# Experts: the late four gated tiles leave in one accumulating store of 1 MB, ahead of GpSimd's norms of the late rows

## The reference, cut to what matters

```
x = x + tanh(g_xattn) * attention(layernorm(x), ctx, ...)      # 4 heads, 64 context rows a batch
x = x + tanh(g_ffn)   * experts(layernorm(x), ...)

experts(x):  grouped  = x.reshape(b, s // 32, 32, d)           # groups of 32 tokens
             logits   = grouped @ Wc + bc + tie                # 128 experts (32 x 4)
             perm     = (logits == max over the 32 tokens)     # each expert takes one token of each group
             permuted = perm^T @ grouped                       # gather
             inner    = relu(permuted @ W1 + b1)               # 512 -> 32 for each expert
             result   = inner @ W2 + b2                        # 32 -> 512
             out      = perm @ result                          # scatter to the tokens
```

## Time and profile before

| | us |
|---|---|
| median of 3 runs | 1733.97 |
| lowest and highest of them | 1730.71, 1737.69 |
| the profiled execution | 1737.52 |
| its span in the trace | 1735.6 |
| PE busy in the span | 1605.5 |
| POOL busy in the span | 861.4 |
| granted TensorE clock, mean | 0.987 |

### The profile page before, as it was taken

One profiled execution on the slowest core, in us unless ns is written; L12 is line 12 of the kernel. 1 busy time (PEld: TensorE's weight loads), 2 busy tenths in 40 slices (PEclk: granted clock), 3 DMA queues, 4 the chain that ended last, 5 costly groups with the idle time before them and its releaser, 6 DMA issues.

```text
span 1735.6 us, 51613 instructions
## 1 busy us (share of the span) xinstructions
PE 1605.5 (93%) x22424; PEld 1126.5 (65%) x22424; DVE 1298.3 (75%) x1893; ACT 739.4 (43%) x966; POOL 861.4 (50%) x1020
## 2 busy tenths in 40 slices
PE   8899999999999999999888998999998889898994
PEld 4677777777777777777676554666555566555662
DVE  5777777777777777777748776778777777776766
ACT  3632323233323333332234555555555455555552
POOL 3468777877787788778641233122233122233122
PEclk9999999999999999999999999999999999999998
DMA  7634545545454455545565888778888787887875
GB/s 290 176 101 151 178 141 174 165 150 164 162 187 138 164 164 163 154 158 170 164 217 174 217 218 223 213 221 202 231 222 220 211 223 191 202 229 210 225 183 153
DMA packets 180593, 325.31 MB, mean 187 GB/s; under 512 B 23056, under 2 KB 33168, under 8 KB 178960
## 3 DMA queue, kind: packets, MB, share of 16 engines
q1 hardware_dynamic: 135104, 239.15, 42.9%
q0 software_dynamic: 17616, 32.52, 11.8%
q10 hardware_dynamic: 27648, 50.34, 8.8%
HBM read 243.23 MB, written 78.71 MB: 185 GB/s over the span
## 4 chain that ended last, share of the span: by engine, by line
PE 61%; DVE 14%; DMA 12%; issue 6%; ACT 3%; POOL 2%; SPq 1%; ACTq 0%; POOLq 0%; DVEq 0%
PE ps L1493 11%; PE ps L951 11%; PE ps L998 10%; PE ps L1463 7%; PE ps L1011 5%; DMA xin<-out 5%; PE ps L1517 3%; PE ps L966 3%; PE ps L1532 3%; DMA out<-xin 3%; PE ps L1024 3%; DMA sel<-lg_scratch 2%; DVE mx L730 2%; DVE res L1405 2%; PE ps L985 2%
## 5 line engine op out<-in xcount | busy, mean ns | idle before, releaser
L184 POOL TENSOR_SCALAR xin<-xin,r_all,nb_all 128x512 f32<-128x512 f32 x128 | 113.7, 891 | 507.3 <-DMA xin<-out 379.5
L1389 DVE STREAM_TRANSPOSE res<-res 128x2048 f32<-128x2048 f32 x128 | 292.0, 2295 | 0.1
L1341 ACT ACTIVATE gat<-ps 128x1536 f32<-128x1536 f32 (+1 forms) x128 | 170.7, 1345 | 204.8 <-PE ps L1463 204.8
L951 PE MATMUL ps<-xTh,qh 128*128 128x512 f32 x512 | 210.3, 411 | 5.6 <-DVE qs L747 2.0
L951 PE MATMUL ps<-xTh,ql 128*128 128x512 f32 x512 | 201.1, 393 | 0.0
L951 PE MATMUL ps<-xTl,qh 128*128 128x512 f32 x512 | 200.5, 392 | 0.0
L1405 DVE COPY res<-ps 128x1024 f32<-128x1024 f32 x128 | 156.7, 1224 | 58.1 <-PE ps L1517 58.0
L1463 PE MATMUL ps<-sel,xin 32*128 32x128 f32 x4096 | 153.7, 285 | 36.6 <-ACT sel L215 10.3
L1312 POOL DMA_DIRECT2D out<-xin x120 | 119.9, 1124 | 97.3 <-DVE xin L1228 85.6
L552 POOL TENSOR_TENSOR xTl<-xT,xTh 128x512 fp32r<-128x512 f32 x128 | 160.5, 1283 | 12.0 <-ACT xTh L616 12.0
L1351 ACT ACTIVATE res<-ps 128x1024 f32<-128x1024 f32 x128 | 131.1, 1025 | 78.4 <-PE ps L1517 78.4
(11 more groups left out here) (169 smaller groups left out, 3288.5 us busy)
## 6 DMA issues: line engine op xcount, KB each, us to landing
gat<-in_W ACTq DMA_DIRECT2D x192, 256.0 KB, 5.6
xT<-in_xT SPq DMA_DIRECT2D x32, 1024.0 KB, 6.1
xin<-in_x SPq DMA_DIRECT2D x64, 512.0 KB, 3.8
out<-xin SPq DMA_DIRECT2D x64, 512.0 KB, 4.0
xin<-out SPq DMA_DIRECT2D x128, 256.0 KB, 4.2
xin<-in_W SPq DMA_DIRECT2D x128, 256.0 KB, 4.0
out<-xin POOLq DMA_DIRECT2D x120, 256.0 KB, 7.3
xT<-in_W SPq DMA_DIRECT2D x68, 256.0 KB, 4.5
```

The lines of the kernel that those rows point to most:

```text
L184: e.tensor_scalar(self.xn[:, t, :], self.xn[:, t, :], self.r[:, i, t:t + 1], self.nb[:, i, t:t + 1], ALU.mult, ALU.add).then_inc(self.m_xn ...
L951: last = e.matmul(ps[:, 2 + n % 2, :], a[:, c, n * DH:(n + 1) * DH], b[:, c, :], start=(k == 0), stop=(k == len(parts) - 1))
L1341: e.activation(o, v, ACT.Copy).then_inc(m_gaA.sem, 1)
L1389: e.transpose(v, v).then_inc(m_tr.sem, 1)
```

## The change

The four separate stores of the late tiles become one of 1 MB with a mark of its own, `d_yn` (`b_yn`). It waits for all four gated tiles, stands behind the wait for the W2 quarter as before, and goes out ahead of the four norms of the late rows. SP's quarters of the middle eighth of W1, and the last load of the late half, wait for that one mark where each waited for the mark of a tile.

```diff
-        d_ys, d_yl = [mark(f"ys{k}", 1, 16) for k in range(NT)], [mark(f"yl{k}", 1, 16) for k in range(2)]
+        d_ys, d_yl = [mark(f"ys{k}", 1, 16) for k in range(NY)], [mark(f"yl{k}", 1, 16) for k in range(2)]
...
+        d_yn = mark("yn", 1, 16)
...
             def load_middle(i, c):
                 if i:
-                    e.wait_ge(d_ys[NY + c].sem, d_ys[NY + c].at(i - 2))
+                    e.wait_ge(d_yn.sem, d_yn.at(i - 2))
...
             def load_last(h):
...
                 for t in range(NY):
-                    k = NY + t if h else t
-                    e.wait_ge(d_ys[k].sem, d_ys[k].at(B - 2))
+                    if h:
+                        e.wait_ge(d_yn.sem, d_yn.at(B - 2))
+                    else:
+                        e.wait_ge(d_ys[t].sem, d_ys[t].at(B - 2))
...
-                for t in range(NY, NT):
-                    if live(i + 1):
+                if live(i - 1):
+                    for t in range(NY, NT):
+                        finished(e, i - 1, t)
+                    e.dma_start(batch(out, i - 1, NY, NY), y, accum_op=ALU.add).then_inc(d_yn.sem, 16)
+                if live(i + 1):
+                    for t in range(NY, NT):
                         route.normed(e, i + 1, t)
-                    if live(i - 1):
-                        add_to_out(i - 1, t)
```

## The result

The changed kernel took 1755.62 us (median of 4 runs, 1748.47 to 1758.38) against 1735.83 us for the kernel before in the same comparison: a ratio of 1.0117, 95% interval 1.0084 to 1.0149. In a second comparison it was 1754.41 us and 1.0134 (1.0107 to 1.0161). Its profiled execution took 1753.85 us, with a span of 1752.0. That is 16.4 us over the span before. The forecast was 1736, with a range to 1753.

What follows compares the result with a forecast made beforehand. PE was taken to set the pace, late norms costing it 6.5 us. Terms of +2.1 us in the rounds and 0 at the end gave 1739.6 profiled, 1736 against the median; 8-in-10 range 1727 to 1753.

Steps and rivals of the forecast that it cites:

- What bounds the kernel: Experts' rounds: PE sets the pace, busy 678 of 750 us; late norms cost it 6.5 us.
- D: Time from the landing of row 4 to that of row 7: mean 4.9 us before, forecast 6.0.
- margins: Per round, time from row 4's landing until gather 1 could start: 4.9 to 10.9 us, each less 1.0 for the norm.
- The 1 MB is in flight while rows 6 and 7 are loaded: Late store competes with both rows: D 6.0 us, ends 5.0 and 7.3; PE waits 8.6 us, +2.1 us.
- loaded rounds: The seven of 14 rounds before the change with D of 5.1 to 7.3 us, mean 6.0.
- rival B: Rows 6 and 7 wait for the whole store: D 9.9 us, waits 58 us, time 1785; chance 0.04.
- A: Rows 6 and 7 come late by their full share of the engines: +11 to +18 us, 1746 to 1752; chance 0.18.
- The issue of the store: On POOL, ahead of the late norms: 3.4 us, hidden unless it takes over 5.3 us.
- Rows 4 and 5 as before: Their loads already compete with early stores and stay at 4.6 us: cost 0.
- The W1 quarters at no cost: On SP, first quarter 2.1 us later, last about as before, with 4.2 us of slack: cost 0.
- The end at 0: Last stores, load and POOL's additions at the kernel's end: 0, within -2 to +2 us.

Runs made afterwards that it cites:

- after_rows_early: The changed kernel with loads of late rows 6 and 7 no longer waiting for those of rows 4 and 5: 1737.76 us, ratio 1.0021.
- four_ahead: The changed kernel with its store split again into four of 256 KB with four marks, at the same place: 1740.77 us, ratio 1.0066.
- one_behind: The changed kernel with its single 1 MB store moved behind the four late norms: 1782.19 us, ratio 1.0292.
- filler: The changed kernel with two dummy gathers between gather 0 and the wait for row 7 in 14 rounds: 1763.03 us, ratio 1.0188.

## Why the prediction was wrong, point by point

- **What bounds the kernel, and D as the quantity that decides:** right. My margins, worked on to D = 8.0, give a wait of 33.3 us; the profile has a mean D of 8.1 and 33.2 us. That the sums agree so closely is in part luck: in the third round the margins give no wait, and PE waited 3.4 us.
- **"The 1 MB is in flight while rows 6 and 7 are loaded":** this step failed. I took D = 6.0, with 7.3 as the end; it was 8.1. So the sum had +2.1 us in the rounds, where PE's wait for the norms grew by 24.9. The range of the whole went no further than 7.3 allows. Both measures that I used were of another kind than what they were to bound. In all loaded rounds row 6 had been issued 0.8 us before the first late store, and row 7 between 0.3 us before it and 0.4 us behind it; and the load of 1 MB at the end was issued 0.3 us behind the first store of only 256 KB. No row of the trace before had a load behind a complete store of 1 MB. after_rows_early shows that this order is worth some 4 us a row. I had weighed the case as rival B and gave it 0.04, by the argument that row 4 lands in 4.6 us among early stores. What came lies between A (1746 to 1752) and B (1785): the rows wait for about 2 to 4 us of the store and then share.
- **Reading the Trainium skill:** "DMA: Bandwidth & Descriptors", Queues, rings and completion order, lets a DMA engine change queues only at packet boundaries. The direction was that of the measurement. But rival B made a turn as large as the store's whole share, and the trace shows no such turn: from 1189 to 1191 the two queues moved 127 and 122 packets. The 2 us before that, in which the loads moved nothing, are not explained by turns, nor by the extent of one store's packets, since with the four stores of four_ahead D was still 7.5. By the Trainium skill's estimate of 4.4 us for 1 MB ("DMA: Bandwidth & Descriptors", Anatomy of one DMA), this store would have been home in time; it took 10.9, and the plain one 6.2.
- **The issue of the store (3.4 us, hidden):** hidden, and only 1.29 us.
- **Rows 4 and 5 as before:** right in that nothing changed. The load of row 4 took 5.6 us in the mean over the 14 rounds before and 5.4 after; the 4.6 us that I used was that of one round.
- **The W1 quarters at no cost:** right for this kernel, as no wait of PE for W1 shows. But the reason was incomplete. "Behind them SP has nothing that PE would miss sooner" is what one_behind refutes: the logits are behind them, and they are missed first.
- **The end at 0:** right, 17.71 against 17.69 us.
- **The clock:** not in the prediction, though the earlier trace rows have it: behind a wait of 2.55 us the gathers took 3.80 us in place of 2.07. PE's waits were priced at their length alone. Behind the long ones the gathers ran at half clock, and their busy time grew by 7.9 us; by filler, how much of that reaches the total is open.

## What to carry to other kernels

Before moving a large store ahead of anything, look at which loads will be issued behind it and what waits for them. Here an accumulating store of 1 MB, issued 1 us sooner than a load of 256 KB, made 3 us into 7; the bytes that stand in front count, not only the bytes in all. A price for contention must be taken from rows where the transfers stand in the same order as they will. And a semaphore that merges four landings into one has a queue behind each of its waiters: follow that queue to the end.

## What the runs showed of the hardware

- An accumulating store of 1 MB in 2 KB rows took 528 packets and 10.9 us (median) to land; the plain one of the same shape 272 and 6.2 us.
- POOL issued such a store of 512 rows in about 1.29 us, against 0.86 at the least for 128 rows.
- Behind the issue of row 7 at 1185.7, with the store issued at 1183.8, SP's queue moved no packet for 2 us; later both queues moved about as many.
- Behind a wait of 4.41 us PE's gathers ran at a granted clock of 0.50, 3.79 us where 2.07 are usual.
